# Top-1 columns on tokens sorted by column with gathered weights, and the near offsets added on TensorE in three 16-bit parts

## What is computed

```python
xn  = layernorm(x)                                # over 256 channels
q, k, v = heads(xn @ W + b)                       # 16 heads of 16
q, k = rotary(q), rotary(k)
att = q @ k.T + rel_bias_table[bucket(i - j)]     # bucket is constant from a distance on
att = where(j <= i, att / 4, -inf)
y   = (softmax(att) @ v) @ Wp + bp
# columns: 16 column nets of 64 neurons, one of them for each token
logits  = cosine(xn, col_emb) + sigmoid(gelu(xn @ w1 + b1) @ w2 + b2)
mask    = one_hot(argmax(logits), 16)             # top_k with k = 1
weights = mask * softmax(logits)
cols    = gelu(einsum('bsd,cdn->bscn', xn, W_cols) + b_cols)
z   = (cols * weights[..., None]).reshape(.., 1024) @ proj_w + proj_b + xn
out = x + y + layernorm(z) * ln_g + ln_b
```

## Time and profile before

| | before |
|---|---|
| median of 3 runs (lowest to highest) | 2119.47 us (2115.34 to 2126.33) |
| profiled execution, its own time | 2120.78 us |
| its span, first to last instruction | 2118.7 us |
| mean granted TensorE clock | 0.962 of full |
| TensorE matmul busy | 1881.9 us, 89% |
| VectorE busy | 1602.9 us, 76% |
| ScalarE busy | 1101.7 us, 52% |
| GpSimd busy | 632.2 us, 30% |
| moved by DMA | 144.77 MB, mean 68 GB/s |

### The profile page before, as it was taken

How to read it: one execution, slowest core, us unless ns; L and a number is a source line. 1 busy time by engine, 2 the same in 40 slices (tenths; PEclk the granted TensorE clock), 3 DMA queues, 4 the chain that set the end, 5 groups by cost and what they waited for, 6 DMA issues and landing times.

```text
span 2118.7 us, 41887 instructions
## 1 busy us (share of the span) xinstructions
PE 1881.9 (89%) x11110; PEld 1051.4 (50%) x11110; DVE 1602.9 (76%) x5859; ACT 1101.7 (52%) x2142; POOL 632.2 (30%) x848
## 2 busy tenths in 40 slices
PE   4887899999999999999999999999999999997677
PEld 2654455555445555555455554455555554443223
DVE  2335788888888688878888778887888788887773
ACT  2231555555565555556555455565555555644444
POOL 5463333223333322233333123333332233300000
PEclk9988899999999999999999999999999999998887
DMA  8422212232222122232212222221222322112101
GB/s 221 130 60 76 59 50 65 56 84 81 66 60 72 49 68 64 60 93 68 59 47 69 70 75 66 65 76 47 70 56 64 86 81 60 47 52 58 45 14 41
DMA packets 199400, 144.77 MB, mean 68 GB/s; under 512 B 60427, under 2 KB 186779, under 8 KB 199148
## 3 DMA queue, kind: packets, MB, share of 16 engines
q1 hardware_dynamic: 199148, 141.85, 24.2%
HBM read 90.59 MB, written 56.69 MB: 70 GB/s over the span
## 4 chain that ended last, share of the span: by engine, by line
PE 58%; DVE 21%; issue 11%; POOL 3%; SPq 3%; ACT 3%; DMA 1%; DVEq 0%; ACTq 0%; POOLq 0%
PE scores L1081 10%; PE bank L1092 9%; PE o_bank L1000 8%; PE scores L983 7%; PE bank L1038 5%; DVE scores L1153 5%; PE rows L1020 4%; DVE rows L1178 4%; PE rows L1026 3%; DVE maxima L1174 3%; PE rows L1024 2%; PE scores L1083 2%; PE bank L1110 2%; DVE maxima L1183 2%; ACT probs L869 2%
## 5 line engine op out<-in xcount | busy, mean ns | idle before, releaser
L869 ACT ACTIVATE probs<-scores 128x512 f32<-128x512 f32 (+1 forms) x1280 | 670.7, 555 | 522.5 <-DVE scores L1153 238.4
L983 PE MATMUL scores<-stack_q,stack_k 99*128 99x512 bf16 (+3 forms) x1536 | 439.0, 337 | 85.2 <-ACT probs L869 60.4
L1178 DVE CUSTOM_DVE_ANT_0 rows<-rows,near_rows 128x256 f32<-128x256 f32 (+1 forms) x1024 | 416.1, 409 | 28.3 <-PE rows L1020 24.6
L1153 DVE TENSOR_TENSOR scores<-scores,near_cols 128x256 f32<-128x256 f32 x768 | 333.6, 443 | 84.5 <-PE scores L983 84.0
L1174 DVE TENSOR_REDUCE maxima<-rows 128x1 f32<-128x256 f32 (+1 forms) x768 | 304.9, 397 | 121.4 <-PE rows L1024 119.3
L1000 PE MATMUL o_bank<-probs,v_aug 128*32 128x512 f32 (+3 forms) x3072 | 320.7, 505 | 3.2 <-ACT probs L869 3.2
L1020 PE MATMUL rows<-stack_k,stack_q 96*128 96x256 bf16 (+1 forms) x1024 | 276.2, 276 | 41.5 <-DVE maxima L1178 24.0
L1081 PE MATMUL scores<-xn_t,w_cols 128*128 128x256 f32 x1024 | 286.9, 404 | 2.5 <-ACT others_t L915 2.5
L1183 DVE TENSOR_REDUCE maxima<-rows 128x1 f32<-128x128 f32 (+3 forms) x512 | 248.9, 486 | 50.3 <-PE rows L1026 48.1
L1092 PE MATMUL bank<-w_proj,act_t 128*128 128x256 f32 x1024 | 270.4, 402 | 16.4 <-DVE y L1211 14.7
L983 PEld LDWEIGHTS scores<-stack_q,stack_k 99*128 99x128 bf16 x1536 | 142.3, 99 | 217.4 <-ACT probs L869 138.1
(11 more groups left out here) (109 smaller groups left out, 2270.2 us busy)
## 6 DMA issues: line engine op xcount, KB each, us to landing
parts_d<-part SPq DMA_DIRECT2D x96, 256.0 KB, 2.5
stack_q<-parts_d SPq DMA_DIRECT2D x384, 64.0 KB, 2.6
stack_k<-parts_d SPq DMA_DIRECT2D x384, 64.0 KB, 2.6
x<-in_x_dram SPq DMA_DIRECT2D x32, 256.0 KB, 3.5
v_d<-v SPq DMA_DIRECT2D x32, 256.0 KB, 2.5
rest_d<-rest SPq DMA_DIRECT2D x32, 256.0 KB, 2.7
v_in<-v_d SPq DMA_DIRECT2D x32, 256.0 KB, 3.3
result<-rest_d SPq DMA_DIRECT2D x32, 256.0 KB, 3.9
```

The lines of the kernel that those rows point to most:

```text
L869: act.activation(probs[:, (g * NS + s) % PROBS, h, 0:width], ring[(rings + ring_n[1]) % RING][:, 0:width], ACT.Exp, scale=float(D) ** -0.5 ...
L983: ins = pe.matmul(ring[(rings + ring_n[1]) % RING][:, c0:c0 + w], stack_k[g % 2][:, h, kb * P:(kb + 1) * P], stack_q[g % 2][:, h, q0:q0 + ...
L1153: dve.tensor_tensor(tile[:, 0:2 * P], tile[:, 0:2 * P], near, ALU.add))
L1178: dve.tensor_tensor_reduce(tile[:, 0:w], tile[:, 0:w], near_rows[:, ag * GH + h, 2 * P - w:2 * P], 1.0, LOWEST, ALU.add, ALU.max, maxima[: ...
```

## The change

- **Sorted tokens.** xn of a whole batch is kept (`xn_all`, with the token's weight as a further element). Once a batch, in group 2, `tally` counts how many tokens chose each column (TensorE sums, some 11 small dependent VectorE steps) and `route` gives each token a slot, each column getting its tokens in blocks of 64 slots. GpSimd scatters the 1024 rows to memory (`xs_d`) with 8 indirect DMAs. 32 blocks of 64 slots a batch (`SLOTS_B` = 2048 slots, padding included) are worked off 8 a group: SyncE loads their tokens, `xs_turn` transposes them, GpSimd's `weights` gathers for each block its own column's weights (128 rows of 385 float32) from a copy `wt_d` with 8 indirect DMAs a group, `neurons` and `columns` multiply each block with its weights alone, ScalarE scales, GpSimd adds xn, SyncE stores. `gather` brings the rows back to token order with 8 indirect DMAs a batch, and the layernorm and the sum with x follow in groups 3 and 0 (`finish_begun`, `finish_stats`, `finish`), x being loaded a second time. `skip`, `rest` and its way through memory go.
- **Near offsets.** `near_cols` is split once into three 16-bit parts (`split`, in the prologue); the score tile gets them by three matmuls with the identity as weights, accumulating. VectorE's part of the score stage and `ring_biased` go.
- **Order.** `CLOSING` keeps `load` alone, the last two pv steps of a group come before the first score of the next (`TAIL`), and `shift` moves to score 34, `shift_turn` to 36.
- **Row tiles** are regrouped: 10 a head in place of 12, near and far ones apart, with 7 plain reduces in place of 10. The rotary work writes its halves directly into `rot`.
- **Setup**: copies of the column weights to memory, a cleared `wt` and `xs_d`, more fills.

```diff
+SLOT = 64
+WROW = KC * N + C + 1
+SLOTS_B = (T // SLOT + E) * SLOT
+FFN_STEPS = NC
+HALVES = SLOTS_B // SLOT // FFN_STEPS
+PAIRS = HALVES // 2
...
+BESIDE = {2: [('widen', None)],
+          3: [('finish_begun', 0)],
+          6: [('center', None), ('finish_stats', 0)],
+          8: [('x_turn', None)],
+          9: [('finish', 0)],
           11: [('qk_begun', 0), ('qk', 0)],
...
+          14: [('xs_turn', 0), ('qk_begun', 1)],
+          15: [('qk', 1)],
+          16: [('xs_turn', 1), ('finish_stats', 1)],
+          18: [('neurons', None), ('hidden', None)],
+          19: [('v', 1), ('finish', 1)],
           21: [('gate', None), ('o_turn', 0)],
+          22: [('columns', 0), ('gather', 1)],
           23: [('qk_turn', 0), ('choose', None)],
+          24: [('columns', 1)],
           25: [('left', 0), ('tie', None), ('middle', 0)],
+          26: [('choice', None), ('y_turn', 0), ('weights', 0)],
+          27: [('weigh', None), ('gather', 0), ('weights', 1), ('qk_turn', 1)],
+          28: [('load_k', None), ('load_v', None), ('project_begun', 0), ('tally', None), ('weights', 2)],
...
+          31: [('middle', 1), ('route', None)],
+          32: [('y_turn', 1), ('weights', 5)],
+          33: [('weights', 6), ('weights_routed', 0), ('weights_routed', 1)],
+          34: [('shift', None), ('project_begun', 1), ('weights', 7), ('weights_routed', 2), ('weights_routed', 3)],
+          35: [('weights_routed', 4), ('weights_routed', 5)],
+          36: [('project', 1), ('shift_turn', None), ('weights_routed', 6), ('weights_routed', 7)],
+          37: [('parts', None)]}
+OPENING = [("again", 0), ("ffn_in", None), ("stats", None)]
...
+CLOSING = [("load", None)]
...
+TAIL = {-2: ("pv", NS - 2), -1: ("pv", NS - 1), 1: ("o_out", 1), 4: ("o_turn", 1)}
...
+                    elif stage == "route":
...
+                        for j in range(NT):
+                            pool.indirect_dma_start(xs_d[:, :], bass.IndirectOffsetOnAxis(slot_i[:, j:j + 1], 0),
+                                                    xn_all[:, j, :], None).then_inc(scattered[j >= CT], 16)
+                    elif stage == "weights":
...
+                        pool.indirect_dma_start(wt[:, arg, :], None, wt_d[:, :],
+                                                bass.IndirectOffsetOnAxis(
+                                                    weight_at[:, k * HALVES + arg:k * HALVES + arg + 1], 0)) \
+                            .then_inc(wt_in, 16)
+                    elif stage == "gather":
...
+                            pool.wait_ge(ys_out, (b + 1) * (FFN_STEPS * 16))
...
+                        for j in range(NT // 2):
+                            at = arg * (NT // 2) + j
+                            pool.indirect_dma_start(gathered_y[:, j, :], None, ys_d[:, :],
+                                                    bass.IndirectOffsetOnAxis(slot_kept[:, at:at + 1], 0)) \
+                                .then_inc(gathered, 16)
...
+                            n0 = max(0, q0 - kb * P)
+                            near = min(2 * P - n0, w)
+                            ins = pe.matmul(tile[:, c0:c0 + w], stack_k[g % 2][:, h, kb * P:(kb + 1) * P],
+                                            stack_q[g % 2][:, h, q0:q0 + w], start=True, stop=near <= 0)
+                            for part in range(3 if near > 0 else 0):
+                                ins = pe.matmul(tile[:, c0:c0 + near], ident_b[:, :],
+                                                near_parts[:, part, g * GH + h, n0:n0 + near],
+                                                start=False, stop=(part == 2))
...
+                        for pair in range(PAIRS):
+                            for h in range(2):
+                                for k in range(KC):
+                                    ins = pe.matmul(tile[h * N:(h + 1) * N, pair * SLOT:(pair + 1) * SLOT],
+                                                    wt[:, pair * 2 + h, k * N:(k + 1) * N],
+                                                    xs_t[:, pair, k, h * SLOT:(h + 1) * SLOT],
+                                                    start=(k == 0), stop=(k == KC - 1))
...
+                                ins = pe.matmul(bank[lanes, q * C:(q + 1) * C], act_t[lanes, 2 * arg + q, :],
+                                                wt[lanes, 2 * (2 * arg + q) + h, KC * N:KC * N + C], start=True, stop=True)
...
-                        if s not in BIASED:
-                            continue
...
-                               dve.tensor_tensor(tile[:, 0:2 * P], tile[:, 0:2 * P], near, ALU.add))
```

More of the change, by code:

```diff
@@ L111 @@
 NORM_STEPS = 5
[L112 to L131 removed]
+ROUTE_STEPS = 14
@@ L142 @@
-          35: [('project_begun', 1)],
-          37: [('project', 1)]}
-OPENING = [("stats", None), ("columns", 0), ("columns", 1), ("columns", 2)]
-ALONE = ([("stats", None), ("center", None), ("x_turn", None)] + [("columns", k) for k in range(C_PIECES)]
-         + [("qk_begun", 0), ("qk", 0), ("qk_begun", 1), ("qk", 1), ("y2_stats", None), ("skip", None),
-            ("hidden", None), ("v", 0), ("gate", None), ("v", 1), ("choose", None), ("qk_turn", 0),
-            ("left", 0), ("tie", None), ("choice", None), ("finish", None), ("middle", 0), ("qk_turn", 1),
-            ("left", 1), ("mask_turn", None)]
-         + [("neurons", (k, m)) for k in range(2) for m in range(N_PIECES)] + [("middle", 1)]
-         + [("neurons", (k, m)) for k in range(2, 4) for m in range(N_PIECES)])
@@ new lines @@
+          33: [('weights', 6), ('weights_routed', 0), ('weights_routed', 1)],
[4 more added lines that the diff above has]
+OPENING = [("again", 0), ("ffn_in", None), ("stats", None)]
+ALONE = [("stats", None), ("center", None), ("x_turn", None), ("qk_begun", 0), ("qk", 0), ("qk_begun", 1), ("qk", 1),
+         ("hidden", None), ("v", 0), ("gate", None), ("v", 1), ("choose", None), ("qk_turn", 0), ("left", 0),
+         ("tie", None), ("choice", None), ("weigh", None), ("middle", 0), ("qk_turn", 1), ("left", 1), ("tally", None),
+         ("route", None)] + [("weights", i) for i in range(HALVES)] + [("middle", 1), ("parts", None)]
@@ new lines @@
+FFN_ALONE = ([("ffn_in", None), ("xs_turn", 0), ("xs_turn", 1), ("neurons", None), ("columns", 0), ("columns", 1)]
+             + [("weights", i) for i in range(HALVES)])
+CLOSING = [("load", None)]
+TAIL = {-2: ("pv", NS - 2), -1: ("pv", NS - 1), 1: ("o_out", 1), 4: ("o_turn", 1)}
+FRONT = {"stats", "center", "x_turn", "qk_begun", "qk", "v", "hidden", "gate", "choose", "tie", "choice",
+         "qk_turn", "weigh", "left", "middle", "parts"}
+ROUTING = {"tally", "route"}
+FFN = {"ffn_in", "xs_turn", "neurons", "columns"}
@@ L211, in add @@
             needs = self.used["hidden"]
+        if stage == "columns":
+            needs = self.used["neurons"]
         if stage == "pv":
-            needs = self.used["score", arg]
+            needs = self.used["score", arg] if g >= 0 else (arg - NS) * GH + GH - 1
         self.stages.append((stage, g, arg, self.banks, self.rings, needs))
@@ L217, in add @@
         self.used[stage, arg[0] if stage == "score" else arg] = self.used[stage]
[L219 to L220 removed]
+        self.banks += stage in BANKED
+        self.rings += ringed
 def iteration(batch):
@@ L256, in iteration @@
         for stage, arg in plan:
-            o.add(stage, g, arg)
+            if stage == "last":
+                o.add(arg[0], g - 1, arg[1])
+            elif stage == "weights_routed":
+                o.add("weights", g, arg)
+            else:
+                o.add(stage, g, arg)
     if batch == B - 1:
+        for at in sorted(TAIL):
+            o.add(TAIL[at][0], NG - 1, TAIL[at][1])
+        o.add("again", NG - 1, NC // 2)
         for k in range(NC // 2, NC):
+            o.add("finish_begun", NG - 1, k)
+            o.add("finish_stats", NG - 1, k)
+            o.add("finish", NG - 1, k)
             o.add("y_turn", NG - 1, k)
```

712 lines of the change are left out of this document (422 added, 290 removed).

## The result

The changed kernel takes 2297.84 us, median of 4 runs (2290.37 to 2300.86), against 2120.31: the ratio is 1.083, with an interval of 1.079 to 1.087. It is 178 us slower, where 1987 us was forecast. The profiled execution took 2300.86 us.

The account below looks back on a forecast made before the run. VectorE was taken to bound the score stretch, TensorE the closing and opening stretch. 6.7 batches at -14.1 us (-94), prologue -35 and tail -5 summed to -134 us from the profiled 2120.78, so 1987 us; range 1880 to 2115.

Parts of the forecast that it names:

- the one under "GpSimd": GpSimd's 48 new gathers and scatters a batch: hidden on average, but a queue stall once a batch costs 4 us.
- c: Cost of one indirect DMA on GpSimd, taken as 1.2 us; stall of 20 x (c - 1.0) us a batch.
- shift wait: New TensorE wait between the turn of the shifts and the first score: 2.0 us a group, bounds 0 and 4.5.
- The freed 4.8 us: TensorE's waits and drains in a group fall from 7.8 to 3.0 us as VectorE loses its additions; bounds nothing and 6.5.
- Rival B: TensorE's waits stay, as it is in order with equal work; 129 us back, 2116 us; chance 0.08.
- 19.6 a batch: Saving over a batch of four groups, from a usual group going from 59.24 to 54.3 us, 4.9 less.
- Prologue: Work before the first group: about 70 us go, 35 come back; net -35, between -50 and -20.
- more early DMAs and fills (5): Prologue term: additional early DMAs and fills add 5 us, part of the 35 us that come back.
- Tail: Last groups: VectorE is relieved, parts and tokens add 15 us to TensorE, finishing chains stand at the end; -5 us.
- A: GpSimd's queue decides: no gain from c = 2.2 us; at 2.5 a 30 us stall a batch, 2161 us; chance 0.13.
- C: Shift path late: its three casts each wait out one gather, 3.6 us; 96 us back, 2083 us; chance 0.11.
- D: More freed: no shift wait or GpSimd stall, fewer waits, cheaper neurons; 1840 us at the extreme, half way 1910; chance 0.18.

Follow-up runs that it names:

- pool_fixed: Changed kernel, its 384 indirect DMAs made plain ones of the same size from and to fixed rows, still issued by GpSimd; 2134.63 us, 1.006 of before.
- near_on_vector: Changed kernel with the near offsets added to the scores by VectorE in float32 again, without TensorE's near-part matmuls; 2288.87 us.
- before_near_on_tensor: Kernel before, with TensorE alone adding the near offsets as three 16-bit parts (second part used twice); 2273.26 us, ratio 1.071.
- the two register versions: Changed kernel with its 256 weight gathers as plain DMAs by a register, and the same with near offsets on VectorE again; 2126.53 and 2104.93 us.
- one_in_flight: Changed kernel, but GpSimd waits before each indirect weight gather until the one before has landed; 2595.41 us.
- weights_register: Changed kernel with the 256 weight gathers as plain DMAs from a place loaded into a register, tokens still indirect; 2126.53 us, ratio 1.004.

## Why the prediction was wrong

The sum was made to 1987 us; 2298 were measured. (The 134 us are taken off the profiled execution; off the median they give 1985.) pool_fixed divides the miss of 311 us. (It ran on chip A; the changed kernel took about the same, 2293 us, on chip C too, and near_on_vector 2289 us on chip A.) The turns of the shifts mark the groups; first and last start in the kernel before, the changed one, and pool_fixed:

```profile
L1068 PE MATMUL bank<-ident_b,shift_p x32: 219/219/313, 217.0 to 2065.7; 128*96 128x128 bf16 x32
```

```profile
L1256 PE MATMUL bank<-ident_b,shift_p x32: 219/228/343, 247.2 to 2234.4; 128*96 128x128 bf16 x32
```

```profile
L1253 PE MATMUL bank<-ident_b,shift_p x32: 219/227/313, 235.5 to 2080.1; 128*96 128x128 bf16 x32
```

| us against before | forecast | pool_fixed | changed |
|---|---|---|---|
| up to the first turn | -35 | +18.5 | +30.2 |
| 31 groups | -94 | -4.1 | +138.5 |
| after the last turn | -5 | +11.5 | +11.7 |
| whole span | -134 | +25.9 | +180.4 |

So about half of the miss is in the late releases, 154.5 us from pool_fixed to the changed kernel, and half was missed without them: 90 us in the groups, 53 in the prologue and 16 in the tail.

**The step that failed** is the one under "GpSimd": it gave the indirect DMAs one price, c, and one way to cost something, as a queue. c was right: 0.96 us and 0.30 to the next, 1.27 against 1.2. The queue did not become late either: at the end of the row of 16 GpSimd waits for VectorE. The price was elsewhere: the 154.5 us of late releases of TensorE, which no term held. The Trainium skill's figure ("DMA: Bandwidth & Descriptors", Latency and other measured facts), about 1 us to the first byte by GpSimd's path, is near the 0.96 us for which an indirect DMA holds GpSimd in this row; it says nothing of what the other engines see.

**TensorE's work.** Right in kind, and too dear on the whole. Near parts 0.11 and 0.06 us apart as counted. Neurons 1.13 us a group from start to start, below the bound of 1.8; columns 2.0 in two pieces (forecast 1.8, bound 3.6): their halves do share the array. Timeline of the changed kernel:

```profile
1121.71 1.20 PE L1268 MATMUL scores<-ys,wt 128*64 128x64 f32 x32
1122.84 0.56 PE L1194 MATMUL rows<-stack_k,stack_q 96*128 96x256 bf16 x3
...
1129.51 1.08 PE L1279 MATMUL bank<-wt,act_t 64*64 64x256 f32 x8 [0.21 <-DVE gate_in L1425]
1130.52 0.56 PE L1194 MATMUL rows<-stack_k,stack_q 96*128 96x256 bf16 x3
```

**A usual group.** 54.3 us was forecast with 2.0 of shift wait. pool_fixed's is 52.3, with 0.8 of shift wait in that group. The freed 4.8 us are borne out by before_near_on_tensor too (5.3). Rival B is refuted for this group.

**But only one group in four is usual.** This is the second failed step: the usual group's 4.9 less was made to "19.6 a batch". From one turn of the shifts to the next the four groups of a batch take 66.9, 59.3, 58.8 and 61.1 us in the kernel before and 68.0, 52.3, 58.9 and 67.3 in pool_fixed: the usual one wins 7.0, the three others lose 1.1, 0.1 and 6.2. In the batch TensorE has 9.9 us less work and is idle 28.8 us, where it was idle 18.1. In the three other groups the path of the tokens adds waits that the forecast had at nothing or at 1.5. Waits of TensorE in pool_fixed, whole span:

```profile
PE bank L1248 <- DMA xs<-xs_d: 71.2, 15, 15.5
...
PE scores L1155 <- DMA stack_q<-shift_t: 25.3, 16, 4.3
PE bank L1236 <- DVE left L1521: 24.8, 8, 3.4
```

The sorted tokens' load is late in two groups of a batch (6.7 and 4.9 us in this one). In the first of them SyncE issues it behind the shifts, the parts and twelve half loads of the stacks, 14.5 us of issuing from 716.61 on:

```profile
722.91 4.59 SPq L673 DMA_DIRECT2D stack_q<-parts_d  x6
...
736.39 0.38 SPq L754 DMA_DIRECT2D xs<-xs_d  x1
```

TensorE is there at 736.9 and gets the tokens at 743.6. I had written that SyncE "loses the rest tile's store and load and gains as much", and called it hidden. That another order would take the wait away was not run. The matmuls of `route` wait 3.1 us for VectorE, the first scores up to 4.3 for the shifts. The granted clock is 0.95 in the two longest groups, where the usual one has 1.00.

**Prologue.** Forecast -35, +18.5 with plain DMAs. Marked by TensorE's first transposes of each chunk's xn, the four steps from chunk to chunk took 30.4, 35.3, 33.3 and 35.2 us in the kernel before and 57.9, 22.0, 21.2 and 35.1 in pool_fixed. The two middle ones gain 13.3 and 12.1 us, where 16 each were forecast; the last is as long as before, as 16 less and 15 more had said. The first loses 27.6 where 14 were to be won: "more early DMAs and fills (5)" was the wrong term. From the last chunk to the first turn it is 16.6 us longer, 15.5 of it one wait for the first sorted tokens, for which tokens and weights had 5 us. In the first step SyncE builds the weight table in DRAM ahead of the offsets. Timelines of SyncE, kernel before and changed:

```profile
12.84 9.06 SPq L558 DMA_DIRECT2D w_cols<-in_W_cols_dram  x2
21.94 2.06 SPq L561 DMA_DIRECT2D b_cols<-in_b_cols_dram  x1
24.19 1.01 SPq L575 DMA_DIRECT2D offsets_d<-rot  x1
```

```profile
17.98 6.18 SPq L640 DMA_DIRECT2D wt_d<-in_proj_w_dram  x1
24.20 4.42 SPq L641 DMA_DIRECT2D wt_d<-in_b_cols_dram  x1
28.66 3.66 SPq L640 DMA_DIRECT2D wt_d<-in_proj_w_dram  x1
32.36 5.81 SPq L641 DMA_DIRECT2D wt_d<-in_b_cols_dram  x1
...
40.92 0.77 SPq L654 DMA_DIRECT2D offsets_d<-rot  x1
```

The offsets leave 16.7 us later, and ScalarE waits 29.7 us for their store (29.1 in pool_fixed, 5.3 in the kernel before), before it copies the first chunk for TensorE. That is about the loss of the first step; I ran no kernel with another order of these loads, so it is read from the trace, not shown by an experiment. The near parts add to the prologue too: without them the first turn comes 12 us earlier (225.7 against 237.5 in the two register versions on chip B).

**Tail.** Forecast -5, +11.5: the finishing chains at the very end were seen, and not priced.

**Rivals.** A came true in sign, not in mechanism; its mechanism exists and is what one_in_flight shows. C: casts of the shift path did not wait out GpSimd's DMAs. The first below takes 0.18 us at 945.79 in the changed kernel, in the middle of the scatters (timeline); the second line has the longest of all 96, 0.42 us (shortest, median and longest of the third cast of each group, in ns). C needed 1.2 each:

```profile
945.79 0.18 DVE L1368 CAST shift_p<-shift 128x32 bf16<-128x32 f32 x1
```

```profile
L1378 DVE CAST shift_p<-shift_l x32: 181/181/419, 246.9 to 2234.0; 128x32 bf16<-128x32 f32 x32
```

By the Trainium skill's rule ("SBUF — State Buffer", Who interferes with whom) VectorE's two-port instructions and GpSimd block each other for a whole instruction. These casts show no such wait beside indirect DMAs; whether they use the shared port at all the trace does not tell, so the rule is neither borne out nor refuted here. D's larger gain exists in the usual group alone.

**What stays open.** Why TensorE's releases, and only TensorE's, arrive late while GpSimd makes indirect DMAs back to back, why the runs on one chip of four show none of it, and whether they would be late without the tracing, whose own records go missing in the same runs. The runs show that the bytes, the packets and the queue are not the cause, and that the pace and the length of the row are part of it.

## What to carry to other kernels

Price a new kind of DMA by what every other engine does while it is made, not only by the time on its own queue: look first for a form without per-row addresses (a register and a plain DMA where the rows are contiguous), and avoid many indirect ones back to back. Count a saving in each kind of group and not in the usual one times four, since the groups that start or end something hold the new waits. Where a path through DRAM is added, follow the issuing queue's order from the first microsecond on, and repeat a comparison on another chip before believing a difference of 1%.

## What the runs showed of the hardware

- TensorE's releases come up to 17.8 us late behind a row of indirect DMAs from GpSimd at 1.27 us each; late ones show on three chips of four (A, C, D). Plain DMAs of the same bytes from the same queue leave none late on A.
- An indirect DMA of 128 rows holds GpSimd for 0.96 us and 0.30 more to the next, whether the rows have 4 or 1540 bytes (0.99 and 0.96); a plain one 0.55 (pool_fixed). With a register load before it, back to back, it is 0.55 too (weights_register, seven in 3.83 us).
- Thirty-two float records of 64 columns took 1.13 us, eight of 256 columns on quarters of the array 1.01.
- TensorE's granted clock falls in the stall and stays down behind it: with TensorE idle from 951.0 on it is 0.52 from 953 to 966.7 (half is 1.2 GHz, 1.00 is 2.4), and at work again from 967.3 it is 0.63 until 972. Three near parts of 256 columns take 0.85 us at 969.14, and 0.49 at 970.97. Over the group it is 0.89.
